# The sine product of the key memory in the phase stage: made by POOL instead of DVE

## The chip, the cores and the metric

The kernel runs on one core of a Trainium2 chip. The metric is the device time of one execution in microseconds (us). The engines are called as in the profile: PE (TensorE) with its weight loads PEld, DVE (VectorE), ACT (ScalarE), POOL (GpSimd) and SP (SyncE, which here only starts transfers).

## The reference, cut to what matters

The model has two layers, each with an attention-like and a feed-forward part, over 8 sequences of 1024 positions and 256 channels. The change lies in the third part, which keeps two running sums over positions. With x normalised and `_shift1` moving the positions back by one, it is:

```python
pos_values = x @ Wpv + bpv
pos_mem_cos = cumsum(pos_cos * pos_values, axis=1)
pos_mem_sin = cumsum(pos_sin * pos_values, axis=1)
pos_ret = (pos_cos * pos_mem_cos + pos_sin * pos_mem_sin) / sqrtD
key_ph = tanh(x @ Wk + bk) * pi
key_cos, key_sin = cos(key_ph), sin(key_ph)
kv_values = x @ Wkv + bkv
gh = gelu(concat([x, _shift1(x)]) @ Wg1 + bg1)
value_gates = sigmoid(gh @ Wg2 + bg2)
kv_mem_cos = cumsum(_shift1(key_cos) * kv_values * value_gates, axis=1)
kv_mem_sin = cumsum(_shift1(key_sin) * kv_values * value_gates, axis=1)
gate_cumsum = maximum(cumsum(value_gates, axis=1), 1.0)
kv_ret = (key_cos * kv_mem_cos + key_sin * kv_mem_sin) / (sqrt(gate_cumsum) * sqrtD)
blended = bw[..., 0:1] * pos_ret + bw[..., 1:2] * kv_ret
return x + layernorm(blended) @ Wo + bo
```

The product that the change moves is `_shift1(key_sin) * (kv_values * value_gates)`.

## The kernel before, in words

The program is a row of stages with a barrier between them: normalise, projections, attention, output projection, routing, experts, phases, slots, combine. Only `phases` is changed (tag `ph`, lines 1394 to 2054). It runs from about 2972 to 3561 us of the profiled span.

In `phases` the 256 channels lie on the partitions in two halves (`mo` = 0 and 1) and the 1024 positions of one sequence `p` along the free dimension, so most tiles are 128x1024 in f32. Each engine has its own instruction order, written out by hand in program order; semaphores tie the engines together, and there is no planner.

- PE makes every projection into four PSUM tiles X, Y, Z, W, used in turn (`products_of` and `SPREAD` fix which product goes into which). `arrived` waits for a product, `gone` waits until its reader has freed it.
- ACT applies gelu, sigmoid, tanh and sine, the roots, and the normalisation of the output.
- DVE does all else: `rotate` (position values times cosine and sine), `key_values` (line 1875 writes `kvg`, the gated values; line 1881 writes `ka` = `kvg` times cosine; line 1882 writes `kb` = `kvg` times sine), `centre` (line 1947), `scan_positions` (lines 1887 and 1888), `scan_keys` (lines 1893 and 1894), `turn_back`, `sum_up` (line 1923 writes the blended result), `gate_sums` (line 1930), `value_weight` (line 1938), and `outputs`, `statistics`, `scales` (line 1982) for the sequence before.
- POOL sets a few constants at the start (lines 1586 to 1592) and then does nothing in the stage.

DVE's order within one pass `p` of its loop (lines 2026 to 2054) is: rotate and key values of half 0, centre of sequence p-1, position scans and key scans of half 0, outputs and statistics of p-1, turn_back of half 0, scales of p-1, sum_up of half 0; then rotate, key values, position scans and key scans of half 1, gate_sums of p+1, turn_back and sum_up of half 1, value_weight of p+1. For p = 0 the half 0 is done ahead of the loop, where no `centre` stands between its products and its key scans. The last pass has neither gate_sums nor value_weight.

A *turn* below is the stretch of DVE from one `value_weight` (line 1938) to the next. Turn p does both halves of sequence p. Turns 1 to 6 begin at 3068.96, 3137.23, 3202.74, 3266.61, 3332.12 and 3395.71 us, and turn 7 at 3459.39 us. Turn 0 is what lies before turn 1, from the gated values at 3021.42 us on.

PE begins its part of a turn with `mean`, whose input is the blended result of line 1923 of the turn before. Behind it PE does `outA`, `outB`, `var`, `k1`, `gh0` and so on without going back to DVE's order. Two things that DVE waits for come down this way: ACT's root of line 1790, which `scales` needs, stands in ACT's order behind the key functions of half 1 and behind `gh0`; ACT's gate values `gt` (line 1738), which `gate_sums` needs, stand behind PE's gate product.

Of the kernel before, what the change touches and what calls it, by code (L numbers as in the profile page):

```python
# [9 lines left out]
ALU = mybir.AluOpType  # L10
# [4 lines left out]
B, T, D = 8, 1024, 256  # L15
NT = T // P
TILES = B * NT
KD = D // P
# [8 lines left out]
FLOOR = 1  # L27
# [1366 lines left out]
def phases(nc, xnT_d, x_d, ppT_d, cols_d, wpv, wk, wkv, wg1, wb1, wo, ident_d, out_d, xn3_d, xnT3_d):  # L1394
# [30 lines left out]
    with Stage(nc, "ph") as st:  # L1425
# [20 lines left out]
        kc = [st.sb(f"kc{mo}", [P, 1 + T]) for mo in range(KD)]  # L1446
        ks = [st.sb(f"ks{mo}", [P, 1 + T]) for mo in range(KD)]
        kvg = st.sb("kvg", [P, T])
        pa = st.sb("pa", [P, T])
        pb = st.sb("pb", [P, T])  # L1450
        ka = st.sb("ka", [P, T])
        kb = st.sb("kb", [P, T])
# [36 lines left out]
        k_ready = st.sem("k_ready")  # L1489
# [4 lines left out]
        w1_ready = st.sem("w1_ready")  # L1494
        rotated = st.sem("rotated")
        m_ready = st.sem("m_ready")
        pos_scanned = st.sem("pos_scanned")
        kv_scanned = st.sem("kv_scanned")
        pos_turned = st.sem("pos_turned")
# [4 lines left out]
        blended = st.sem("blended")  # L1504
# [17 lines left out]
        def arrived(eng, product):  # L1522

            eng.wait_ge(made[bank[product]], FLOOR + turn_of[product] + 1)

        def gone(eng, product):

            eng.wait_ge(freed[bank[product]], FLOOR + turn_of[product] + 1)

        with st.block() as block:  # L1530
# [52 lines left out]
            @block.gpsimd  # L1583
            def _(pool):
                for j in range(2):
                    pool.memset(xT[j][:, :, 0:1], 0.0)
                for mo in range(KD):
                    pool.memset(kc[mo][:, 0:1], 0.0)
                    ins = pool.memset(ks[mo][:, 0:1], 0.0)
                ins.then_inc(zeroed, 1)  # L1590
                pool.memset(avg[:], 1.0 / D)
                pool.memset(avg16[:], 1.0 / D / 16).then_inc(zeroed, 1)

            @block.tensor
            def _(pe):
# [258 lines left out]
            def _(dve):  # L1854
# [12 lines left out]
                def key_values(mo, p):  # L1867

                    u, name = 2 * p + mo, f"kv{mo}"
                    arrived(dve, (name, p))  # L1870
                    if mo == 0:
                        gone(dve, ("gate", p))
                    if u >= 1:
                        dve.wait_ge(m_ready, FLOOR + u)
                    STT(kvg[:], flat[bank[name, p]], column(BKV + mo), gt[:], ALU.add, ALU.mult
                        ).then_inc(freed[bank[name, p]], 1)
                    gone(dve, (name, p))
                    dve.wait_ge(k_ready, FLOOR + u + 1)
                    if u >= 1:
                        dve.wait_ge(blended, FLOOR + u)  # L1880
                    dve.tensor_tensor(ka[:], kvg[:], kc[mo][:, 0:T], ALU.mult)
                    dve.tensor_tensor(kb[:], kvg[:], ks[mo][:, 0:T], ALU.mult).then_inc(m_ready, 1)

                def scan_positions(mo, p):

# [4 lines left out]
                def scan_keys(mo, p):  # L1890

                    dve.wait_ge(m_ready, FLOOR + 2 * p + mo + 1)
                    dve.tensor_tensor_scan(ka[:], ones[:], ka[:], 0.0, ALU.mult, ALU.add)
                    dve.tensor_tensor_scan(kb[:], ones[:], kb[:], 0.0, ALU.mult, ALU.add).then_inc(kv_scanned, 1)

                def turn_back(mo, p):
# [124 lines left out]
                scan_positions(0, 0)  # L2021
                gate_sums(0)
                key_values(0, 0)
                scan_keys(0, 0)
                value_weight(0)
                for p in range(B + 1):
                    if 1 <= p < B:
                        rotate(0, p)
                        key_values(0, p)
                    if p >= 1:  # L2030
                        centre(p - 1)
                    if 1 <= p < B:
                        scan_positions(0, p)
                        scan_keys(0, p)
                    if p >= 1:
                        outputs(p - 1)
                        statistics(p - 1)
                    if p < B:
                        turn_back(0, p)
                    if p >= 1:  # L2040
                        scales(p - 1)
                    if p < B:
                        sum_up(0, p)
                        rotate(1, p)
                        key_values(1, p)
                        scan_positions(1, p)
                        scan_keys(1, p)
                    if p + 1 < B:
                        gate_sums(p + 1)
                    if p < B:  # L2050
                        turn_back(1, p)
                        sum_up(1, p)
                    if p + 1 < B:
                        value_weight(p + 1)
# [431 lines left out]
def build_program(nc, a, out):  # L2486

    def scratch(name, shape):
        return nc.dram_tensor(name, shape, F32, kind="Internal").ap()

    x0, ident = a["x"], a["ident"]
    xn, xnT = scratch("xn", (B * T, D)), scratch("xnT", (KD, P, B * T))
    xn3, xnT3 = scratch("xn3", (B * T, D)), scratch("xnT3", (KD, P, B * T))
    qk, v, ctxT = scratch("qk", (B, 2, H, HD, T)), scratch("v", (B * T, D)), scratch("ctxT", (B, D, T))
    den, rden = scratch("den", (B, H, T)), scratch("rden", (B, H, T))
    x1, x3 = (scratch(n, (B * T, D)) for n in ("x1", "x3"))
    wt = scratch("wt", (P, 2, B * E))
    idx = nc.dram_tensor("idx", (P, 2, B * E), U32, kind="Internal").ap()
    y = scratch("y", (B, NP, D))
    lg = scratch("lg", (B * T, NP))  # L2500

    normalise(nc, "n0", x0, None, xnT, ident)
    qkv_rope(nc, xnT, a["wqk"], a["bqk"], a["L0_attn_Wv"], a["L0_attn_bv"], a["cos"], a["sin"], qk, v)
    attend(nc, qk, v, ident, a["kaug"], ctxT, den, rden)
    project(nc, "pj", ctxT, a["L0_attn_Wo"], a["L0_attn_bo"], x0, x1)
    normalise(nc, "n1", x1, xn, xnT, ident)
    route(nc, xnT, a["L0_ffn_gate_w"], ident, a["rowbase"], idx, wt)
    experts(nc, xn, idx, wt, a["L0_ffn_Wg"], a["L0_ffn_Wu"], a["L0_ffn_Wd"], ident, a["L1_attn_Wo"], a["L1_attn_ln_b"],
            a["L1_attn_bo"], x1, xnT)
    phases(nc, xnT, x1, a["ppT"], a["cols"], *(a["L1_attn_" + n] for n in ("Wpv", "Wk", "Wkv", "Wg1", "Wb1", "Wo")), ident,  # L2510
           x3, xn3, xnT3)
    soft_slots(nc, xn3, xnT3, a["phi"], a["L1_ffn_W"], a["L1_ffn_b"], y, lg)
    soft_combine(nc, lg, y, ident, x3, out)
# [29 lines left out]
```

## Time and profile before

| | us |
|---|---|
| median of 3 runs | 5219.01 |
| lowest, highest | 5214.22, 5226.11 |
| the profiled execution, its own time | 5225.51 |
| its span | 5223.7 |

| engine | busy us | share of the span |
|---|---|---|
| PE | 4665.9 | 89% |
| PEld | 3086.4 | 59% |
| DVE | 3280.5 | 63% |
| ACT | 2126.9 | 41% |
| POOL | 1122.6 | 21% |

A busy share is a mean over stages with different limits, so the table doesn't say what bounds the phase stage; its own stretches do. In the rows below, a timeline row gives start and duration, and in brackets how long the engine sat idle before the instruction and whose work ended that. A row without brackets began without such a wait. An `x8` or `x2` at its end means that so many instructions were merged into the row. PEclk is TensorE's granted clock as a share of full speed.

### The profile page before, as it was taken

To read this page: it belongs to the slowest core of one execution; us is meant where nothing else is said; L and a number is where in the kernel's file an instruction comes from. 1 tells how busy PE (TensorE), PEld (TensorE's weight loads), DVE (VectorE), ACT (ScalarE), POOL (GpSimd) and SP (SyncE) were. 2 spreads that over 40 slices of the span, in tenths; PEclk is the share of its full clock that TensorE was granted. 3 is DMA by queue.
4 is the path that set the end of the run, shared out by engine and by line. 5 is a ranking of instruction groups with operands and counts; after the bars stand their busy time and mean duration, and the time that the engine had idled before them with its cause. 6 is when DMAs were issued, how large, how long until landed. Compare 5 with 4: busy or idle time off the path is not lost. (4 is left out here: it accounts for less than half of the span.)

```text
span 5223.7 us, 71222 instructions
## 1 busy us (share of the span) xinstructions
PE 4665.9 (89%) x27922; PEld 3086.4 (59%) x28080; DVE 3280.5 (63%) x3853; ACT 2126.9 (41%) x3473; POOL 1122.6 (21%) x850
## 2 busy tenths in 40 slices
PE   5969999999999965399999699976999999979999
PEld 3512222222322234288888445446999999968888
DVE  5668888888888814612222389994776666644443
ACT  1027767776766721022222255542222222223333
POOL 1431222122122020044444100001333333310000
PEclk9969999999999985599999899988999999989999
DMA  6644434443443268053434312217444444455553
GB/s 217 186 74 64 63 66 77 73 79 64 72 84 62 36 190 308 30 150 80 88 80 89 103 48 81 81 65 213 100 98 98 101 99 98 98 164 188 187 174 121
DMA packets 458704, 568.05 MB, mean 109 GB/s; under 512 B 29793, under 2 KB 373217, under 8 KB 450017
## 3 DMA queue, kind: packets, MB, share of 16 engines
q1 hardware_dynamic: 261728, 405.44, 29.9%
q10 hardware_dynamic: 172160, 125.85, 10.3%
q0 software_dynamic: 24576, 33.57, 3.9%
q8 instruction: 150, 2.46, 0.2%
q14 instruction: 90, 0.73, 0.1%
HBM read 286.74 MB, written 227.67 MB: 98 GB/s over the span
## 5 line engine op out<-in xcount | busy, mean ns | idle before, releaser
L743 DVE TENSOR_REDUCE att_nmx<-att_s 128x1 f32<-128x1024 f32 x1024 | 1205.4, 1219 | 237.8 <-PE att_s L653 234.1
L729 ACT ACTIVATE att_pt<-att_sT 128x512 f32<-128x512 f32 x2048 | 1059.4, 604 | 481.5 <-PE att_sT L670 307.2
L653 PE MATMUL att_s<-att_KT,att_QT 96*128 96x512 bf16 x2048 | 793.0, 391 | 65.2 <-DMA att_KT<-att_hi 37.8
L670 PE MATMUL att_sT<-att_QT,att_KT 128*128 128x512 bf16 x1890 | 720.6, 384 | 6.8 <-ACT att_pt L729 6.7
L2156 POOL TENSOR_TENSOR sl_lg<-sl_lg,sl_sm 128x512 f32<-128x512 f32 x256 | 319.6, 1269 | 1319.8 <-DVE sl_sm L2294 1319.8
L670 PEld LDWEIGHTS att_sT<-att_QT,att_KT 128*128 128x128 bf16 x2048 | 197.7, 97 | 652.8 <-ACT att_pt L729 441.5
L684 PE MATMUL att_o<-att_pt,att_va 128*32 128x512 f32 x4096 | 555.4, 609 | 0.0
L2167 PE MATMUL sl_lp<-sl_phi,sl_xT 128*128 (+1 forms) x4160 | 491.8, 277 | 31.9 <-DMA sl_xT<-xnT 24.0
L2167 PEld LDWEIGHTS sl_lp<-sl_phi,sl_xT 128*128 128x128 f32 x4160 | 479.2, 193 | 38.8 <-issue 38.8
L2407 PE MATMUL cb_op<-cb_y,cb_exT 128*128 128x256 f32 x2048 | 485.5, 380 | 0.0
L2205 PE MATMUL sl_acc<-sl_lg,sl_xn 128*128 128x128 f32 x4096 | 478.3, 275 | 0.0
L2205 PEld LDWEIGHTS sl_acc<-sl_lg,sl_xn 128*128 128x128 f32 x4096 | 467.7, 192 | 0.0
L2227 ACT ACTIVATE sl_lg<-sl_lg 128x1024 f32<-128x1024 f32 x128 | 135.3, 1057 | 763.5 <-DVE sl_lg L2283 763.5
L1356 DVE TENSOR_TENSOR moe_hT<-moe_sg,moe_up 128x512 f32<-128x512 f32 x128 | 88.0, 688 | 533.5 <-PE moe_yp L1221 325.4
L2407 PEld LDWEIGHTS cb_op<-cb_y,cb_exT 128*128 128x128 f32 x2048 | 370.8, 191 | 40.0
L653 PEld LDWEIGHTS att_s<-att_KT,att_QT 96*128 96x128 bf16 x2048 | 199.1, 99 | 247.3 <-DVE att_nmx L743 50.6
L2292 DVE TENSOR_REDUCE sl_sm<-sl_lg 128x128 f32<-128x1024 f32 x128 | 248.6, 1942 | 136.5 <-ACT sl_lg L2227 136.5
L1154 POOL DMA_INDIRECT x<-moe_y,moe_idx x128 | 213.2, 1666 | 345.0 <-ACT moe_y L1272 325.5
L579 POOL COPY att_QT<-att_QT 32x1024 bf16<-32x1024 bf16 x64 | 72.7, 1162 | 923.1 <-DVE att_QT L764 922.9
L1207 PE MATMUL moe_gp<-moe_xT,moe_wg 128*128 128x256 f32 x1024 | 244.0, 382 | 1.7 <-DVE moe_bo L1374 0.9
L1207 PE MATMUL moe_up<-moe_xT,moe_wu 128*128 128x256 f32 x1024 | 243.1, 380 | 0.0
L1221 PE MATMUL moe_yp<-moe_wd,moe_hT 128*128 128x256 f32 x1024 | 231.6, 379 | 1.4 <-DVE moe_hT L1356 1.4
(251 smaller groups left out, 5985.4 us busy)
## 6 DMA issues: line engine op xcount, KB each, us to landing
lg<-sl_raw ACTq DMA_DIRECT2D x128, 512.0 KB, 5.7
cb_ex<-lg SPq DMA_DIRECT2D x64, 1024.0 KB, 6.2
sl_w<-in_L_ffn_W SPq DMA_DIRECT2D x68, 256.0 KB, 3.7
xnT<-n_xnT ACTq DMA_DIRECT2D x32, 512.0 KB, 5.0
qk<-qkv_turned ACTq DMA_DIRECT2D x64, 256.0 KB, 3.2
att_qin<-qk SPq DMA_DIRECT2D x64, 256.0 KB, 9.1
y<-sl_y SPq DMA_DIRECT2D x16, 1024.0 KB, 7.3
cb_y<-y SPq DMA_DIRECT2D x8, 2048.0 KB, 8.5
```

Of the source, the lines that this page charges most:

```text
L653: ins = pe.matmul(s[i % 2][:, c, :], QT[n % NB][0:ROWS, h, t * P:(t + 1) * P], KT[n % NB][0:ROWS, h, c * 512:(c + 1) * 512], start=True, s ...
L670: pe.matmul(sT[:, idx % 3, :], KT[g % NB][:, h, kt * P:(kt + 1) * P], QT[g % NB][:, h, step // 4 * 512:(step // 4 + 1) * 512], start=True, ...
L684: ins = pe.matmul(o[32 * h:32 * h + 32, :], va[g % 2][:, kt, h, :], pt[:, step % 2, h, c, :], start=kt == 0, stop=kt == NT - 1)
L729: act.activation(pt[:, step % 2, h, c, :], sT[:, idx % 3, :], ACT.Exp, scale=HD ** -0.5).then_inc(exp_done, 1)
L743: dve.tensor_reduce(nmx[n % 2][:, t, h:h + 1], s[i % 2][:].rearrange("p c k -> p (c k)"), AX.X, ALU.max, negate=True).then_inc(freed, 1)
L1207: ins = pe.matmul(o_[:, m, :], w_[:, k, (2 * h + m) * P:(2 * h + m + 1) * P], xT[n % 2][:, k, :], start=k == 0, stop=k == KD - 1)
L1221: ins = pe.matmul(yp[n % 2][:, s, :], hT[m // 2][:, m % 2, s * P:(s + 1) * P], wd[e][:, m, :], start=m == 0, stop=m == NI - 1)
L2156: pool.tensor_tensor(part_, part_, sm[j][:].rearrange("p (a n) -> p a n", a=1).broadcast_to([P, HB, P]), ALU.mult).then_inc(shared, 1)
L2167: ins = pe.matmul(lp[j][:, b, :], xT[:, k, b * T + m * P:b * T + (m + 1) * P], ph[:, k, bass.ds(c * P, P)], start=k == 0, stop=k == KD - 1)
L2205: ins = pe.matmul(acc[:, k, b, :], xn[:, b * NT + m, k * P:(k + 1) * P], lg[m % 4][:, b, :], start=m == 0 and b % 4 == 0, stop=m == NT - 1 ...
L2292: ch.link(dve.tensor_reduce(sm[j][:], lg[l][:].rearrange("p b n -> p n b"), AX.X, ALU.add))
L2407: ins = pe.matmul(op[n % 2][:], exT[n % 2][:, s, :], y[b % 2][:, s, :], start=s == 0, stop=s == SK - 1)
```

## The change

The sine product leaves DVE's `key_values` and becomes POOL's only work in the stage behind its constants. POOL walks through the same sequences and halves. Before each product it waits until `kvg` is written (`gone`), until the keys of this half are ready (`k_ready`), and until `kb` is no longer read (`blended`). It signals a new semaphore, `by_sine`. DVE waits for it ahead of the scan over `kb` and ahead of the next writing of `kvg`.

```diff
+        by_sine = st.sem("by_sine")
...
+                def sine_products(mo, p):
+
+                    u, name = 2 * p + mo, f"kv{mo}"
+                    gone(pool, (name, p))
+                    pool.wait_ge(k_ready, FLOOR + u + 1)
+                    if u >= 1:
+                        pool.wait_ge(blended, FLOOR + u)
+                    pool.tensor_tensor(kb[:], kvg[:], ks[mo][:, 0:T], ALU.mult).then_inc(by_sine, 1)
+
+                for p in range(B):
+                    for mo in range(KD):
+                        sine_products(mo, p)
...
                     if u >= 1:
                         dve.wait_ge(m_ready, FLOOR + u)
+                        dve.wait_ge(by_sine, FLOOR + u)
...
-                    dve.tensor_tensor(ka[:], kvg[:], kc[mo][:, 0:T], ALU.mult)
-                    dve.tensor_tensor(kb[:], kvg[:], ks[mo][:, 0:T], ALU.mult).then_inc(m_ready, 1)
+                    dve.tensor_tensor(ka[:], kvg[:], kc[mo][:, 0:T], ALU.mult).then_inc(m_ready, 1)
...
                     dve.tensor_tensor_scan(ka[:], ones[:], ka[:], 0.0, ALU.mult, ALU.add)
+                    dve.wait_ge(by_sine, FLOOR + 2 * p + mo + 1)
                     dve.tensor_tensor_scan(kb[:], ones[:], kb[:], 0.0, ALU.mult, ALU.add).then_inc(kv_scanned, 1)
```


## Rows read from the trace of the kernel before

**Rows 1.** Turns 2 and 5: us; busy PE, PEld, DVE, ACT, POOL; PEclk; DMA share, GB/s.

```profile
3137.23:3202.74 65.51, 62.59 (x188) 33.67 (x188) 63.41 (x70) 36.17 (x38) 0.00 (x0) 0.95 0.24 81
3332.12:3395.71 63.59, 59.25 (x188) 31.62 (x188) 63.18 (x69) 36.16 (x38) 0.00 (x0) 1.00 0.25 83
```

**Rows 2.** Timeline of PE, head of turn 3: start us, us, engine, line, operation.

```profile
3202.87 2.41 PE L1606 MATMUL ph_psZ<-ph_bl,ph_avg 128*128 128x512 f32 x5 [2.58 <-DVE ph_bl L1923]
```

**Rows 3.** Timeline of DVE: the reciprocal of line 1982, turns 1, 2, 3, 5, 6, 7.

```profile
3102.66 0.20 DVE L1982 RECIPROCAL ph_nrstd<-ph_nrstd 128x8 f32<-128x8 f32 x1 [4.12 <-ACT ph_nrstd L1790]
...
3168.17 0.20 DVE L1982 RECIPROCAL ph_nrstd<-ph_nrstd 128x8 f32<-128x8 f32 x1 [1.34 <-ACT ph_nrstd L1790]
...
3232.25 0.20 DVE L1982 RECIPROCAL ph_nrstd<-ph_nrstd 128x8 f32<-128x8 f32 x1
...
3361.62 0.20 DVE L1982 RECIPROCAL ph_nrstd<-ph_nrstd 128x8 f32<-128x8 f32 x1
...
3425.22 0.19 DVE L1982 RECIPROCAL ph_nrstd<-ph_nrstd 128x8 f32<-128x8 f32 x1
...
3488.90 0.20 DVE L1982 RECIPROCAL ph_nrstd<-ph_nrstd 128x8 f32<-128x8 f32 x1
```

**Rows 4.** Timeline of ACT: the root of line 1790, turns 3, 5, 6, 7.

```profile
3231.70 0.30 ACT L1790 ACTIVATE ph_nrstd<-ph_mv,ph_eps 128x8 f32<-128x8 f32 x1
...
3359.39 0.30 ACT L1790 ACTIVATE ph_nrstd<-ph_mv,ph_eps 128x8 f32<-128x8 f32 x1
...
3424.49 0.30 ACT L1790 ACTIVATE ph_nrstd<-ph_mv,ph_eps 128x8 f32<-128x8 f32 x1
...
3487.88 0.30 ACT L1790 ACTIVATE ph_nrstd<-ph_mv,ph_eps 128x8 f32<-128x8 f32 x1
```

**Rows 5.** Timeline of DVE: the scan of line 1930, turns 1 and 3.

```profile
3123.95 2.29 DVE L1930 TENSOR_TENSOR_SCAN ph_cs<-ph_ones,ph_gt 128x1024 f32<-128x1024 f32 x1 [0.36 <-ACT ph_gt L1738]
...
3253.33 2.29 DVE L1930 TENSOR_TENSOR_SCAN ph_cs<-ph_ones,ph_gt 128x1024 f32<-128x1024 f32 x1 [0.16 <-ACT ph_gt L1738]
```

**Rows 6.** Timeline of DVE, turn 3: start us, us, engine, line, operation.

```profile
3206.26 1.27 DVE L1875 SCALAR_TENSOR_TENSOR ph_kvg<-ph_psX,ph_col,ph_gt 128x1024 f32<-128x1024 f32 x1
3207.57 1.23 DVE L1881 TENSOR_TENSOR ph_ka<-ph_kvg,ph_kc 128x1024 f32<-128x1024 f32 x1
3208.71 1.22 DVE L1882 TENSOR_TENSOR ph_kb<-ph_kvg,ph_ks 128x1024 f32<-128x1024 f32 x1
3209.85 2.34 DVE L1947 SCALAR_TENSOR_TENSOR ph_sq<-ph_bl,ph_psZ 128x1024 f32<-128x1024 f32 x2
3212.11 2.28 DVE L1887 TENSOR_TENSOR_SCAN ph_pa<-ph_ones,ph_pa 128x1024 f32<-128x1024 f32 x1
...
3243.20 1.22 DVE L1882 TENSOR_TENSOR ph_kb<-ph_kvg,ph_ks 128x1024 f32<-128x1024 f32 x1
3244.34 2.28 DVE L1887 TENSOR_TENSOR_SCAN ph_pa<-ph_ones,ph_pa 128x1024 f32<-128x1024 f32 x1
```

**Rows 7.** Timeline, attention stage: POOL and DVE, one stretch.

```profile
709.28 4.50 POOL L599 TENSOR_TENSOR att_num<-att_num,att_rb 128x2048 f32<-128x2048 f32 x1 [31.74 <-DMA att_num<-ctxT]
709.42 4.44 DVE L755 TENSOR_TENSOR att_naug<-att_nrest,att_naug 128x32 bf16<-128x32 f32 x1
```

**Rows 8.** Lines 755 and 579: duration ns min/median/max, first and last start us, forms.

```profile
L755 DVE TENSOR_TENSOR att_naug<-att_nrest,att_naug x32: 226/227/4446, 334.9 to 1818.0; 128x32 bf16<-128x32 f32 x32
L579 POOL COPY att_QT<-att_QT x64: 1034/1078/1317, 338.2 to 1820.8; 32x1024 bf16<-32x1024 bf16 x64
```

**Rows 9.** Group of line 866: busy us, mean ns, idle before.

```profile
L866 POOL TENSOR_TENSOR pj_x<-pj_x,pj_bias 128x1024 f32<-128x1024 f32 x16 | 37.6, 2347 | 41.5 <-DMA pj_x<-in_x 26.8 <-DMA pj_bias<-in_L_attn_bo 14.7
```

**Rows 10.** Timeline, projection stage: DVE and POOL, one stretch.

```profile
98.07 0.74 DVE L333 SCALAR_TENSOR_TENSOR qkv_by_sin<-qkv_mm,qkv_bqk,qkv_sin 128x512 f32<-128x512 f32 x1
98.89 1.26 POOL L350 TENSOR_TENSOR qkv_turned<-qkv_by_cos,qkv_by_sin 128x512 f32<-128x512 f32 x1 [98.43 <-DVE qkv_by_sin L333]
99.42 0.75 DVE L332 SCALAR_TENSOR_TENSOR qkv_by_cos<-qkv_mm,qkv_bqk,qkv_cos 128x512 f32<-128x512 f32 x1 [0.61 <-PE qkv_mm L311]
```

## The prediction, made before the changed kernel was timed

> **What bounds the kernel now.** The page's chain of waits runs only through the combine stage at the end, so for the phase stage I read, in this order: the windows by turn, the waits at the head of a turn, and the places where DVE itself waits. The windows show DVE busy 63.41 of 65.51 us in turn 2 and 63.18 of 63.59 us in turn 5, PE 62.59 and 59.25 us, POOL nothing [rows 1]. DVE is the fuller engine, but PE is close behind, so the second question is who waits for whom. PE stands idle 2.58 us at the head of turn 3, until DVE's blended result is there [rows 2]. So DVE starts each of PE's turns. The other way round, DVE waits twice in a turn for what PE and ACT made from that start: at the reciprocal of line 1982 for ACT's root (4.12 us in turn 1, 1.34 in turn 2, and alike in turn 4; no wait in turns 3, 5, 6, 7) [rows 3], and at the scan of line 1930 for the gate values (0.36 us in turns 1, 2 and 4, 0.16 in turn 3, none in 5 and 6) [rows 5]. There are two loops of nearly one length: DVE's own work, and PE's chain from the blended result to root and gates. A microsecond off DVE counts only where DVE is the later one; a microsecond onto DVE counts nearly everywhere.
>
> How much later DVE is at line 1982 comes from its start less the end of ACT's root and 0.03 us of hand-over (turn 1: 3102.33 + 0.30 to 3102.66): turn 3: 3232.25 - 3232.03 = 0.22 us; turn 5: 1.90; turn 6: 0.40; turn 7: 0.69 [rows 3, 4]. In turns 1, 2 and 4 it is nothing. The gates come 21.3 us behind the root (turn 1: 3123.95 - 3102.66; turn 3: 3253.33 - 3232.03), and DVE needs 20.9 us from line 1982 to line 1930 (21.3 less its wait of 0.36) [rows 3, 5].
>
> **The change part by part.** *Removed from DVE:* 16 products. The next instruction starts 1.14 us behind such a product (3208.71 to 3209.85, 3243.20 to 3244.34) [rows 6], so 2 x 1.14 = 2.28 us a turn.
>
> *Added to POOL:* 16 products of two f32 tiles of 128x1024. The nearest rows are those of line 866, same shape, both inputs f32 in SBUF: 2.35 us each [rows 9]. POOL has nothing else in the stage, so for POOL alone this would be free.
>
> *What the two do to each other.* POOL's 4.50 us product with two SBUF inputs began at 709.28 us. DVE's little product, two SBUF inputs as well, began at 709.42 and took 4.44 us, where its median is 0.227: it ended with POOL's, at 713.8 [rows 7, 8]. So such a DVE instruction does not share; it stands still until POOL is through. The other way, a POOL copy that starts beside a DVE copy takes up to 1.317 us for 1.034, so POOL stands behind a running DVE instruction too [rows 8]. No such loss shows where DVE has one input in PSUM: its multiply of 0.74 us takes 0.75 beside POOL's product [rows 10]. The Trainium skill (SBUF — State Buffer, Who interferes with whom) says the same, and more widely: any DVE instruction with two SBUF inputs contends with a GpSimd instruction that reads SBUF, and the later one to issue is blocked whole. By that rule the scans, which read `ones` and the product, are blocked too; no row of before has a scan beside POOL.
>
> *Who comes first.* DVE's cosine product starts 0.04 us behind the end of `kvg` (3206.26 + 1.27 to 3207.57) [rows 6]; POOL starts 0.08 us behind a DVE result (98.07 + 0.74 to 98.89) [rows 10] and has three waits to go through. So I take DVE as first: POOL's product starts to run when the cosine product ends, 1.2 us later.
>
> *Half 0, turns 1 to 7.* Behind the cosine product come the two instructions of `centre`, with one input in PSUM, 2.26 us until the next starts (3209.85 to 3212.11) [rows 6]. POOL's 2.35 us, of which some 0.1 passes while it stands in line, lie beside them. Cost about nothing, at most 0.1 us; without that cover it would be the 1.2 us of half 1. DVE reaches line 1982 by 1.14 us sooner, and what is late there next is ACT's root: only 0.22 + 1.14 + 0.40 + 0.69 = 2.45 us of the gain are kept, in turns 3, 5, 6, 7, and nothing in 1, 2, 4.
>
> *Half 1, turns 0 to 7, and half 0 of turn 0.* Nothing from PSUM stands between: the cosine product is followed by scans back to back, all with two SBUF inputs [rows 6]. POOL's 2.3 us have to be inserted somewhere in DVE's row: ahead of the first scan if POOL gets its turn there, or at the new wait ahead of the scan over `kb`, where a hand-over of 0.08 us comes on top. Behind the waiting scan stand gate_sums, turn_back, sum_up, and with them PE's next `mean`. Cost: 2.3 - 1.14 = 1.2 us, nine times, 10.8 us. Bounds: if the scans don't contend, it is a gain of 1.14; if POOL ran beside DVE's cosine product, it would end 2.43 us behind `kvg`, 1.2 behind that product, and the cost would be 0; with all of POOL's row and slow hand-overs 1.4.
>
> From the nine come off the waits at line 1930 that are filled: 3 x 0.36 + 0.16 = 1.24 us.
>
> *Other added work.* DVE's wait ahead of `kvg` is for a product scanned long before. One more semaphore is raised by POOL at the stage's start: under 0.1 us. Nothing but DVE reads `kb`, and no transfer moves.
>
> Sum: 10.8 - 2.45 - 1.24 = +7.1 us. The profiled execution's own time of 5225.5 would be 5232.6; it lies 6.5 us above the median of the runs, and 5219.0 + 7.1 = 5226 us.
>
> The size hangs on PE's clock. Turn 5, all at full granted clock, gets the root early; turn 2, at 0.95, gets it 1.34 us later than DVE is ready for it, and is 1.9 us longer [rows 1, 3]. If every turn went like 2, the kept gains and slacks of turns 3, 5, 6, 7 would be gone and the sum would be about +15 us; if every one went like 5, about 0. PE's idle time at a turn's head grows from 2.58 to some 3.4 us, which speaks more for the upper side.
>
> **The rivals.**
>
> *POOL first (slower).* If POOL begins ahead of the cosine product at half 0, DVE stands still for its whole 2.35 us there and `centre` hides nothing. DVE then comes to line 1982 by 1.2 us later instead of 1.14 sooner. It decides where PE's chain leaves less than that: in turns 3, 5, 6 and 7 (in 1 and 2 the waits of 4.12 and 1.34 cover it). There the kept 2.45 us turn into losses of nearly 1.2 each: 7.1 + 2.45 + 4.6 = +14 us, 5233 us. For it: the two starts are only 0.04 us apart. Against: POOL's three waits, and DVE's smaller hand-over.
>
> *The scans don't contend.* The sine product is wholly hidden, DVE gains 2.28 us a turn. But PE's chain holds: nothing is gained in turns 1, 2, 4, next to nothing in 3 and 6 (DVE now comes to line 1930 with no or a little wait), 1.5 in turn 5 (1.90 less the 0.4 by which 21.3 exceeds 20.9), 0.69 + 1.14 in turn 7, and up to 2.3 in turn 0: -5.5 us, 5213.5 us. For it: no row shows a scan beside POOL. Against: it has two SBUF inputs like the blocked product. A scan also takes 2.2 us where a product takes 1.14 [rows 6], so it might read only half the time and leave room in between; nothing shows that. The Trainium skill (DVE: opcode table, instruction layouts, handler registers and perf-mode slots; Datapath and trigger behaviour) has the scan run at half throughput, with which these two times agree.
>
> *POOL runs beside the cosine product.* Half 1 costs 0 and the gain of half 0 is kept only in turns 5 and 7: 1.1 + 0.7, so -2 us, 5217 us. Against: the delayed copies of rows 8.
>
> **How the numbers follow.** Forecast 0.60, POOL first 0.13, scans free 0.13, side by side 0.14. A measurement of this kernel can tell 0.2%, 10.4 us, from no change. The forecast's own range is 5219 to 5234 us by the clock term; within it I give slower by over 0.2% (above 5229.4) a quarter, 0.15. Of POOL first two thirds are slower, 0.09. Of the scans' case, a third with PE's idle time and clock going its way would reach below 5208.6: 0.04, and 0.01 more for the rest. So faster 0.05, same 0.71, slower 0.24. The runs of before alone spread over 12 us, so the range goes from 5211 to 5238.
>
> **What would show it.** After: line 1882 gone from DVE, 16 POOL rows out of `kvg`; at half 0 of turns 1 to 7 a POOL row of about 3.4 us (1.1 in line, 2.3 of work) with `centre` at 2.35 as before; at half 1 either a first scan of 4.5 us instead of 2.28, or a gap of about 2.4 us on DVE ahead of the scan over `kb`, released by POOL. DVE's wait at line 1982 should now appear in all turns but about one or two, the waits at line 1930 should be gone, and turns should be about 0.8 us longer at the same clock. I am wrong if DVE's scans keep 2.2 us beside a running POOL product, if the cosine product takes 3.5 us, or if the phase stage gets shorter by more than 5 us.

## The result and the profile after

The changed kernel took 5224.8 us (median of 22 runs, 5216.4 to 5236.0), the kernel before 5211.6 us in its 22 (5206.6 to 5226.1; the three runs shown first were high for it). The ratio is 1.0027, interval 1.002 to 1.0034, which is 14 us (10 to 18). The profiled execution of after took 5224.59 us, that of before 5225.51, so the two traces hardly differ in length and can only show the mechanism, not the size.

The windows of two turns of after answer to [rows 1]: turn 2 (the common kind) and turn 4 (TensorE at full granted clock all through). Columns as there.

```profile
3130.47:3194.70 64.23, 60.76 (x188) 32.26 (x188) 63.16 (x68) 36.16 (x38) 6.79 (x2) 0.97 0.25 82
3262.28:3325.75 63.47, 59.07 (x188) 31.69 (x188) 63.06 (x68) 36.16 (x38) 6.79 (x2) 1.00 0.25 83
```

POOL is busy 6.79 us a turn, yet DVE's busy time at full clock went only from 63.18 to 63.06 us, although two products of 1.22 us had left it. The busy share doesn't tell work from standing still: a blocked instruction counts as busy. The timeline of after shows where the removed time went. These are half 1 of turn 3 and half 0 of turn 4, to be read beside [rows 6]; the POOL rows are put behind DVE's of the same place.

```profile
3236.99 1.22 DVE L1895 TENSOR_TENSOR ph_ka<-ph_kvg,ph_kc 128x1024 f32<-128x1024 f32 x1
3238.13 4.43 DVE L1900 TENSOR_TENSOR_SCAN ph_pa<-ph_ones,ph_pa 128x1024 f32<-128x1024 f32 x1
3242.49 2.26 DVE L1901 TENSOR_TENSOR_SCAN ph_pb<-ph_ones,ph_pb 128x1024 f32<-128x1024 f32 x1
...
3237.03 3.38 POOL L1601 TENSOR_TENSOR ph_kb<-ph_kvg,ph_ks 128x1024 f32<-128x1024 f32 x1 [34.05 <-DVE ph_kvg L1889]
...
3267.11 1.23 DVE L1895 TENSOR_TENSOR ph_ka<-ph_kvg,ph_kc 128x1024 f32<-128x1024 f32 x1
3268.25 2.34 DVE L1961 SCALAR_TENSOR_TENSOR ph_sq<-ph_bl,ph_psZ 128x1024 f32<-128x1024 f32 x2
3270.51 2.28 DVE L1900 TENSOR_TENSOR_SCAN ph_pa<-ph_ones,ph_pa 128x1024 f32<-128x1024 f32 x1
...
3267.15 3.41 POOL L1601 TENSOR_TENSOR ph_kb<-ph_kvg,ph_ks 128x1024 f32<-128x1024 f32 x1 [26.74 <-DVE ph_kvg L1889]
```

In both halves the POOL product begins 0.04 us behind the cosine product and lasts 3.4 us: one part in line behind it, the rest at work. In half 1 the next DVE instruction is a scan with two SBUF inputs. It takes 4.43 us for 2.28, because it stands still until POOL is through, and the next scan can only start 4.36 us behind it instead of 2.20. In half 0 the next one is `centre`, which reads PSUM; it keeps 2.34 us, and the scan behind it keeps 2.28. The per-line rows say that this is so throughout (duration ns min/median/max):

```profile
L1900 DVE TENSOR_TENSOR_SCAN ph_pa<-ph_ones,ph_pa x16: 2280/3357/4443, 2998.2 to 3493.9; 128x1024 f32<-128x1024 f32 x16
L1906 DVE TENSOR_TENSOR_SCAN ph_ka<-ph_ones,ph_ka x16: 2256/2260/4327, 3019.4 to 3500.5; 128x1024 f32<-128x1024 f32 x16
```

The median of line 1900 lies midway between the two durations: eight scans are long, eight short. Of line 1906 one is long, that of half 0 of sequence 0. That makes the nine collisions of the prediction.

What DVE gains in half 0 shows mostly as a wait. Over the stage it waits at the reciprocal seven times in after where before it was four times [rows 3]. The total hardly differs (7.4 for 7.2 us), because it depends on how many turns ran at a lower clock in that execution; the number of waits tells more. At the gates' scan all waits of [rows 5] are gone; what is left is the one in the stage's head. PE's `mean` at the head of a turn [rows 2] waits longer, 46.4 us for 40.7 over eight. First before, then after (the columns are us in total, times, longest):

```profile
DVE ph_cs L1930 <- ACT ph_gt L1738: 8.5, 5, 7.3
DVE ph_nrstd L1982 <- ACT ph_nrstd L1790: 7.2, 4, 4.1
PE ph_psZ L1606 <- DVE ph_bl L1923: 40.7, 8, 19.0
...
DVE ph_cs L1944 <- ACT ph_gt L1751: 6.7, 1, 6.7
DVE ph_nrstd L1996 <- ACT ph_nrstd L1803: 7.4, 7, 4.0
PE ph_psZ L1619 <- DVE ph_bl L1937: 46.4, 8, 20.0
```

### The profile page after: what moved, and what is told of

The parts are those of the page before. It is cut to its first block and busy times, and to the rows that moved or that the text cites. A ratio compares the mean times of both kernels' runs of the same rounds, so it can differ in the third digit from the quotient of the medians.

```text
span 5222.5 us, 71246 instructions
## 1 busy us (share of the span) xinstructions
PE 4657.3 (89%) x27922; PEld 3084.2 (59%) x28080; DVE 3279.4 (63%) x3837; ACT 2126.6 (41%) x3473; POOL 1176.8 (23%) x866
```

## The experiments

Times below are compared in two ways. The ratio is to runs of before that were timed beside each group of experiments. The second way uses `b1` and `b2`, copies of the kernel before run as experiments: they read 1.0010 and 1.0018 instead of 1.000, so the ratio flatters before by about 7 us. Part of it can be seen: the runs of before lie at two levels. Beside `b2` six of its 29 took 5219.7 to 5225.6 us and the other 23 took 5205.6 to 5215.0, while all eleven of `b2` took 5218.4 to 5229.2. What decides between the levels isn't known. Means over all runs in experiments: copies of before 5223.3 us (22 runs), changed kernel 5227.7 us (24 runs). Differences of means to those 22 runs are called *like for like*; their 95% intervals come from resampling the runs. `b1`, `e4`, `e5` and `e7` ran on one chip, all others, `b2` among them, on another.

**a1_change_again and a2_change: the changed kernel, no edit.**

> The changed kernel once more, for a second profile and for times beside the kernels sent with it. Blocking theory: each POOL product that meets scans stops DVE for about 2.1 us where the removed product took 1.1, so nine times +1.0 us, less what waits on PE and ACT absorb: +5 to +10 us on before by this account, of which the first measurement (+13, interval 10 to 18) shows more. Clock theory: the rest of the +13 comes from more turns in which TensorE's granted clock falls; then this profile has two or more turns of the phase stage longer than 65.5 us. Layout theory: the rest comes from outside the phase stage; then the phase stage from the first gated values to the last blended result takes 498 to 500 us as in both first profiles.

> The changed kernel, to be read against b2_before in the same call and with as many runs, since a copy of the kernel before, sent as an experiment, read 1.0010 and not 1.000. Blocking theory with the measured 1.0 us a collision: +5 to +9 us against b2_before. If the first +13 was right as it stood: +11 to +16 against b2_before.

Measured: 5227.1 us, ratio 1.0024 (1.0015 to 1.0033), and 5229.5 us, 1.0024 (1.0015 to 1.0032). Like for like +4.5 us (1.8 to 7.1) for both together; the 22 runs of the first measurement, taken the same way, give +3.3 (0.4 to 6.2). Against `b2` alone, as a2's expectation had it, a2 is +3.7 us (0.3 to 6.9): the centre lies below the expected +5 to +9, and the +11 to +16 of the other case is out. From the first gated values to the last blended result the three profiles of the change took 498.4, 501.9 and 505.4 us, mean 501.9. The three of before average 499.5 (below), so the stage shows +2.4, with a spread of 7 between executions; the six profiled executions as a whole show +5.5, with a spread of as much. So most of the first +13 came from what it was compared with, and the layout theory has little left to explain; e1 below tests it.

**b1_before_again and b2_before: the kernel before, no edit.**

> The kernel before, sent as an experiment, for a second profile and as a null comparison. The first profile of before was taken at 5225.5 us, 14 above the median of its runs. Clock theory: a run at the median has nearly only turns of 63.6 us in the phase stage, where the first profile had one of 68.3 and two of 65.5; so a profile nearer 5212 shows fewer long turns, and ratio 1.000. Layout theory: the phase stage takes the same 498 to 499 us in it and the difference lies in other stages.

> The kernel before, sent as an experiment once more, as the ruler for the other three. Ratio to the runs of before 1.000 to 1.001.

Measured: 5224.1 us, 1.0010 (1.0001 to 1.0019), and 5224.9 us, 1.0018 (1.001 to 1.0027). A copy of the kernel before reads slower than the kernel before, so a ratio of this size can't be taken as the size of a change. The same stretch of the phase stage took 498.7, 499.7 and 500.0 us in the three profiles of before, with turns of 63.6 to 63.9, 65.5, 67.0 and 68.0 to 68.3 us mixed differently each time. The clock theory says that an execution at the median of 5212 us would be nearly free of long turns. No execution that fast was profiled: b1's took 5221.0 us and had three of them, as many as the first, at 5225.5. The theory stays open.

**e1_signals: all waits and signals, no product on POOL.**

```diff
-                    pool.tensor_tensor(kb[:], kvg[:], ks[mo][:, 0:T], ALU.mult).then_inc(by_sine, 1)
+                    pool.sem_inc(by_sine, 1)
...
-                    dve.tensor_tensor(ka[:], kvg[:], kc[mo][:, 0:T], ALU.mult).then_inc(m_ready, 1)
+                    dve.tensor_tensor(ka[:], kvg[:], kc[mo][:, 0:T], ALU.mult)
+                    dve.tensor_tensor(kb[:], kvg[:], ks[mo][:, 0:T], ALU.mult).then_inc(m_ready, 1)
```

> POOL goes through all its waits and raises by_sine at once, but multiplies nothing; DVE makes both products as in the kernel before and keeps the added waits. Blocking theory: no difference from before (within 3 us), scans 2.27 us, the product of line kb back on DVE. Layout theory (the added waits, the new semaphore or the longer program cost the time): +8 to +14 us as in the changed kernel.

Measured: 5223.0 us, 1.0016 (1.0007 to 1.0024). By the ratio alone this looked like most of the loss. Like for like it is -0.4 us (-2.4 to 2.1): waits, signals and program length cost nothing that these runs can tell. The scans keep their time (first scan 2282 ns on average).

**e2_half0 and e3_half1: only the products of one half on POOL.** The edit chooses by a condition, and DVE makes the others:

```diff
+        by_pool = lambda mo, p: mo == 0 and p >= 1      # e3_half1: mo == 1
+        pool_units = [(mo, p) for p in range(B) for mo in range(KD) if by_pool(mo, p)]
...
+                    if not by_pool(mo, p):
+                        ins = dve.tensor_tensor(kb[:], kvg[:], ks[mo][:, 0:T], ALU.mult)
```

> POOL makes the sine product only for half 0 of sequences 1 to 7, where centre with its PSUM input follows; DVE makes the other nine. Blocking theory: no scan is stopped, POOL rows of 3.4 us beside centre, DVE 1.14 us earlier at the reciprocal of nrstd, where it waits for ACT in nearly all turns: -1 to -3 us on before (kept gain 2.45 by the first profile). Rival (DVE alone sets the turn): 7 x 1.14 = -8 us. Rival (PE's chain sets all): 0.

> POOL makes the sine product only for half 1 of all eight sequences, where scans follow; DVE makes the half-0 ones. Blocking theory: first position scan of half 1 takes 4.4 us instead of 2.28, 8 x 1.0 us less up to 1.2 absorbed at the gates' scan: +6 to +8 us on before, so the whole loss of the changed kernel (and a little more, as half 0's gain is missing) sits here. Rival (the loss is spread over all sixteen products, by waits and signals): half of it, +6 us with e2 also at +5 or more.

Measured: e2 5219.1 us, 1.0006 (0.9996 to 1.0016), like for like -4.3 us (-8.5 to -0.1). e3 5234.3 us, 1.0035 (1.0025 to 1.0045), like for like +9.7 us (5.8 to 13.2). The two halves have opposite signs, as the blocking theory says, and the spread-out rival falls. The times of e2 alone are weak evidence, since five of its twelve runs lie at 5209.7 to 5214.3 us and the other seven at 5218.4 to 5229.6; its turns say more, and e3's interval is clear of 0. The per-line row of e3 has the eight long scans, and none at the key scans, as sequence 0's half 0 is back on DVE:

```profile
L1907 DVE TENSOR_TENSOR_SCAN ph_pa<-ph_ones,ph_pa x16: 2280/3358/4444, 3000.8 to 3504.1; 128x1024 f32<-128x1024 f32 x16
L1913 DVE TENSOR_TENSOR_SCAN ph_ka<-ph_ones,ph_ka x16: 2257/2260/2291, 3023.4 to 3510.6; 128x1024 f32<-128x1024 f32 x16
```

In e2 a turn at full granted clock took 62.45 us, where before took 63.59 [rows 1]: the whole 1.14 us is kept. A turn at 0.95 took 65.33 for 65.51, and one at 0.92 took 67.02 for the 67.04 of `b2`. There DVE waits at the reciprocal, 14.5 us over the stage, twice as long as in before: most of the 8.0 us taken off it is handed to that wait (in this execution, the slowest of e2's twelve). Columns as in [rows 1]:

```profile
3202.79:3265.24 62.45, 59.07 (x188) 31.68 (x188) 62.04 (x69) 36.18 (x38) 3.41 (x1) 1.00 0.25 84
3137.46:3202.79 65.33, 62.41 (x188) 33.64 (x188) 62.25 (x69) 36.17 (x38) 3.41 (x1) 0.95 0.24 81
```

```profile
L2004 DVE RECIPROCAL ph_nrstd<-ph_nrstd 128x8 f32<-128x8 f32 x8 | 1.6, 199 | 14.5 <-ACT ph_nrstd L1806 14.5
```

**e5_both_make: POOL's product comes on top, saving nothing.** The product goes into a tile that nothing reads, and DVE makes both of its own:

```diff
+        idle = st.sb("idle", [P, T])
...
+                    pool.tensor_tensor(idle[:], kvg[:], ks[mo][:, 0:T], ALU.mult).then_inc(by_sine, 1)
```

> DVE makes both products as before, and POOL makes the sine product once more into a tile that nobody reads, with all waits of the changed kernel. This is the cost of POOL's company alone, nothing saved. Blocking theory: POOL is in line behind two DVE products (rows of about 4.5 us), then stops the first scan by 2.1 us in half 1 and in turn 0, is covered by centre otherwise: nine times +2.1 = about +19 us on before, scans of 4.4 us in the same places. Rival (scans share the port): 0.

Measured: one run, 5255.2 us; the stretch of the phase stage took 529.3 us, 30 more than before, where I had expected about 19. The mechanism held, my picture of who waits didn't. I expected POOL in line behind both DVE products and covered by `centre`; the timeline of turn 3 shows it behind the first only:

```profile
3214.78 1.23 DVE L1896 TENSOR_TENSOR ph_ka<-ph_kvg,ph_kc 128x1024 f32<-128x1024 f32 x1
3214.83 3.39 POOL L1602 TENSOR_TENSOR ph_idle<-ph_kvg,ph_ks 128x1024 f32<-128x1024 f32 x1 [27.87 <-DVE ph_kvg L1890]
3215.93 3.37 DVE L1897 TENSOR_TENSOR ph_kb<-ph_kvg,ph_ks 128x1024 f32<-128x1024 f32 x1
3219.22 2.34 DVE L1963 SCALAR_TENSOR_TENSOR ph_sq<-ph_bl,ph_psZ 128x1024 f32<-128x1024 f32 x2
```

DVE's second product takes 3.37 us for 1.22, all sixteen do (mean 3375 ns), and the scans are untouched. So the waiting engine gets its turn at the end of the instruction it waited for, though DVE's next one stands ready. Sixteen times 2.15 is 34 us, less some wait at the gates. In every case seen, the DVE instruction that pays is the one directly behind the cosine product, if both its inputs are in SBUF.

**e7_order_only: the order of e4 on the kernel before.**

```diff
-                        rotate(0, p)
                         key_values(0, p)
+                        rotate(0, p)
...
-                        rotate(1, p)
                         key_values(1, p)
+                        rotate(1, p)
```

> The kernel before with the same reordering as e4_covered (key_values ahead of rotate in both halves from sequence 1 or half 1 on), nothing on POOL. It separates the order from the move to POOL. Blocking theory: 0, within 4 us, since DVE's row is as full as before. Rival (the order itself is what helps or hurts e4_covered): the same sign and size as e4_covered.

Measured: 5226.0 us, 1.0011 (1.0001 to 1.0021), like for like -0.3 us (-4.4 to 3.5). The order alone makes no difference that these runs can tell.

**e4_covered: the change with that order.** The same edit on the changed kernel: behind the cosine product now comes `rotate`, which reads PSUM.

> The change, with key_values ahead of rotate on DVE in both halves (except half 0 of sequence 0), so that DVE's two PSUM-reading products follow the cosine product and POOL's product has them beside it. Blocking theory: scans keep 2.27 us except the first key scan of sequence 0; DVE's own work is 2.28 us a turn shorter than before, but the gate values now bind: a turn at full clock 62.2 us for 63.6, so -5 to -10 us on before, and 15 to 20 us below the changed kernel. Rival (the loss of the change comes from added waits, signals or program length): +5 to +10 us, as POOL and all signals are the same.

Measured: 5219.8 us, 1.0005 (0.9996 to 1.0014), like for like -4.1 us (-6.7 to -1.5), against `b1` alone, on the same chip, -3.0 (-6.2 to 0.6). That is a little short of the expected 5 to 10 below before, and some 8 us below the changed kernel, where I had expected 15 to 20, which fits only the ratio's +13 for the changed kernel. All collisions but sequence 0's half 0 are gone:

```profile
L1900 DVE TENSOR_TENSOR_SCAN ph_pa<-ph_ones,ph_pa x16: 2281/2288/2293, 2997.6 to 3491.6; 128x1024 f32<-128x1024 f32 x16
L1906 DVE TENSOR_TENSOR_SCAN ph_ka<-ph_ones,ph_ka x16: 2261/2265/4336, 3020.3 to 3496.0; 128x1024 f32<-128x1024 f32 x16
...
L1944 DVE TENSOR_TENSOR_SCAN ph_cs<-ph_ones,ph_gt 128x1024 f32<-128x1024 f32 x8 | 18.3, 2288 | 15.5 <-ACT ph_gt L1751 15.5
L1996 DVE RECIPROCAL ph_nrstd<-ph_nrstd 128x8 f32<-128x8 f32 x8 | 1.6, 201 | 10.3 <-ACT ph_nrstd L1803 10.3
```

DVE now stands 25.8 us at the two places that PE's chain feeds, where it was 8.5 + 7.2 in before. The turn at full clock was 61.98 us for 63.59, so there 1.6 of the 2.28 us taken off DVE are kept.

**e8_covered_chain and e9_chain_only: PE's chain shortened, with and without POOL.**

```diff
-                + [(n, p + 1) for n in ("gh1", "bh") if ahead] + [(n, p - 1) for n in ("trA", "trB") if last]
-                + [(n, p + 1) for n in ("gate", "z", "k0", "kv0", "pv0") if ahead])
+                + [(n, p + 1) for n in ("gh1", "bh", "gate") if ahead] + [(n, p - 1) for n in ("trA", "trB") if last]
+                + [(n, p + 1) for n in ("z", "k0", "kv0", "pv0") if ahead])
...
-                    if p + 1 < B:
-                        front("gh0", p + 1)
                     if p >= 1:
                         norm_deviation(p - 1)
                         normal(p - 1)
                     if p + 1 < B:
+                        front("gh0", p + 1)
                         front("gh1", p + 1)
                         front("bh", p + 1)
+                        gates(p + 1)
                     if p >= 1:
                         take_turned(p - 1)
                     if p + 1 < B:
-                        gates(p + 1)
                         shares(p + 1)
```

In PE's own loop `gate(p + 1)` moves ahead of the two `turn` calls in the same way. e8 has beside it the order of e4, and leaves the sine product of sequence 0's half 0 to DVE.

> As e4_covered, with half 0 of sequence 0 left to DVE (nothing from PSUM to cover it), and with PE's chain shortened: PE's gate product ahead of the two transposes, ACT's root and normalisation ahead of the gelu of gh0, ACT's gates ahead of the copies of the transposes. Two-loops theory (what POOL saves on DVE was eaten by the root and the gates that come down PE's chain): DVE's waits at the reciprocal and at the gates' scan all but vanish, a turn is 61.4 us of DVE's own work for 63.6, -12 to -20 us on b2_before. Rival (PE itself, 60 us busy in a turn, or its clock is the floor): turns stay at 62 to 65 us, -3 to -8 us as e4_covered.

> The kernel before with the shortened chain of e8_covered_chain alone, POOL idle. Two-loops theory: DVE's 63.5 us are now the length of every turn, the longer ones of 65.5 and 67 to 68 us go: -4 to -9 us on b2_before. Rival (PE's clock makes the turn long whatever DVE waits for): 0, and long turns remain.

Measured: e8 5190.6 us (5 runs, 5187.9 to 5200.1), ratio 0.9947 (0.9935 to 0.996), like for like -31 us (-35 to -27). It beats both kernels, and by more than the expected 12 to 20. e9 5218.9 us, 1.0003 (0.9994 to 1.0011), like for like -6.3 us (-9.7 to -3.0). e9 is as expected (4 to 9 below). Against `b2` alone, as the expectations had it, they are -32 and -7.5 us. Two turns of e8, turn 3 of e9, and e8's two waits over its stage:

```profile
3127.64:3189.09 61.45, 60.53 (x188) 32.56 (x188) 61.01 (x67) 34.78 (x38) 6.80 (x2) 0.97 0.26 86
3189.09:3252.16 63.07, 62.23 (x188) 33.15 (x188) 61.13 (x68) 34.71 (x38) 6.79 (x2) 0.95 0.25 84
...
3196.40:3260.00 63.60, 62.37 (x188) 33.71 (x188) 63.19 (x70) 34.79 (x37) 0.00 (x0) 0.95 0.25 83
```

```profile
L1951 DVE TENSOR_TENSOR_SCAN ph_cs<-ph_ones,ph_gt 128x1024 f32<-128x1024 f32 x8 | 18.2, 2272 | 8.7 <-ACT ph_gt L1754 8.7
L2003 DVE RECIPROCAL ph_nrstd<-ph_nrstd 128x8 f32<-128x8 f32 x8 | 1.6, 198 | 0.4 <-ACT ph_nrstd L1806 0.4
```

Five of e8's six full turns are 61.4 us, DVE's own work, as expected. The sixth, turn 3 at a granted clock of 0.95, is 63.1 with PE busy 62.2 of it: there PE's work is nearly the whole turn, as the rival had it, and the wait at the gates that is left (1.5 us there, the rest in the head of the stage) is its sign. In e9 five of six are 63.6 us, that of 0.95 too, where before took 65.51 at 0.95. So the long turns of before weren't set by PE's clock alone, but by the waits that a slower PE put into DVE. That is also why my 12 to 20 us was too low: it compared 61.4 with the 63.6 of a good turn, but before's six full turns average 65.2 us in its three profiles, and e8's 61.7.

The two gains are not additive: e4 alone saves 4, the chain alone 6, both 31. The phase stage accounts for the profiled execution: from first gated values to last blended result it took 475.5 us, 24 less than the 499.5 of before's three profiles, and the execution as a whole, 5200.1 us, is 23 below the mean of theirs (5223.4). It was the slowest of e8's five; the other four, 5187.9 to 5192.6 us, have no profile, so where their further 7 to 12 us come from isn't known.

## Why the prediction was right, and where it wasn't

- *POOL's product and DVE's two-input instructions exclude each other, scans too:* right, by after, e3 and e5. The rival that scans are free is out, and so is the one that POOL runs beside the cosine product: its row would then be 2.35 us long [rows 9], and all 16 are 3.38 to 3.41.
- *DVE goes first, POOL starts when the cosine product ends:* right, in all 16, by 0.04 to 0.05 us. POOL got there sooner than I thought, so its three waits cost nearly nothing and the margin is thin. What POOL first would cost was not tried.
- *Half 0 of turns 1 to 7 is covered by `centre`:* right; where DVE doesn't wait, it comes to the reciprocal 28.37 us into the turn for 29.51, exactly the 1.14 saved.
- *Collision +1.2 us:* mis-sized. In the stretch from the reciprocal to the gates' scan DVE needs 21.86 us in after for 20.84 in before, so +1.02. I had 2.3 us of POOL work in DVE's way; the scan is 2.15 us longer. Nine times that is 9.2, not 10.8, and the sum would have been +5.5.
- *The gain is handed to the wait on ACT's root:* right as a mechanism (e2, after): with the chain shortened the same DVE time comes back (e8).
- *The sum, +7.1 us:* like for like +4.5 (1.8 to 7.1); by the given ratio +14 (10 to 18). Turn by turn at the same clock the difference is 67.6 for 67.0, 64.2 for 63.7, 63.5 for 63.6, and in turn 0 49.4 for 47.5 us; that is 1.9 and some 0.4 for most of the others, near 5. I had foreseen 0.8 for a turn; at full clock it is -0.1, as half 0 keeps its whole 1.14 and half 1 costs 1.02. The slacks I read off turns 3, 5, 6 and 7 were one execution's mixture of clocks; in the other profiles of before the waits fall in turns 1, 4 and 5. The same reckoning there gives kept gains of 3.8 and 2.9 us for my 2.45, so the size was near, but it was not a property of those turns.
- *The time, 5226 us:* that 5224.8 was measured is luck in part. I added +7.1 to 5219.0, the median of three runs that was 7.4 above the median of the 22. The measured difference between the two medians is 13.2, so the base was too high by about as much as the difference was too low.
- *The chances:* no change had 0.71. The comparison made first says slower by 0.27%, beyond the 0.2% of the prediction; like for like it is slower by 0.09%, within it. The step that was too sure was taking a bound of 0.2% as clear of noise, when a copy of a kernel can read 0.18% above its original.
- *The clock term, about 15 us if all turns go like turn 2:* open, and its two ends don't follow from the terms named for them: 7.1 plus the kept 2.45 and the slacks of 3.2 is 12.8, not 15; and with 1.14 kept in all seven turns 10.8 - 8.0 is 2.8, not 0. PE's idle time at the head of a turn grew from 2.58 to 3.12 us, and long turns (over 65.4 us) were one, two and three in after's three profiles, three, three and three in before's. The guess that more idle time gives more long turns has no support here.

## What to carry to other kernels

Before moving an elementwise product from DVE to POOL, look at the DVE instructions that follow the moment POOL becomes ready, for as long as POOL will work. In this kernel two of them with one input in PSUM (2.3 us together) covered a POOL product of 2.3 us, and the move was free; where one with two SBUF inputs came first, DVE paid 2.15 us to save 1.14. Putting PSUM readers there cost nothing that could be measured (e7). A single PSUM reader, shorter than POOL's work, was not tried. Then look for the second loop. Here most of the time taken off the fuller engine was eaten by waits that the other engine's chain put into it: both edits together gave 31 us, each alone 4 and 6.

## What the runs showed of the hardware

- A POOL product of two f32 tiles of 128x1024 in SBUF and a DVE scan of the same shape hardly overlap, although the scan takes 2.18 us for 1024 columns where a product takes 1.14: the scan beside POOL took 4.43 us for 2.28. By the rule of the Trainium skill (SBUF — State Buffer, Who interferes with whom) the second of the two to issue blocks whole until the first has finished; the traces agree with it for scans as for products.
- The turn passes to the waiting engine between two DVE instructions issued back to back, in all 16 cases of e5 (mean of the blocked product 3375 ns) and at the nine places of after.
- Beside a DVE instruction with one input in PSUM nothing is lost: the two of `centre` kept 2.34 us, and in e4 `rotate` in their place left all scans but one at 2.26 to 2.29 us.
- A POOL product of 2.35 us alone [rows 9] shows as 3.4 us when it waits for a DVE product; its row alone doesn't say that it waited.
- The same kernel, timed as before and as an experiment, differed by 0.10% and 0.18%, both intervals clear of 1.
- With PE's order and work unchanged, a turn of before took from 63.6 to 63.9 us, at a granted clock of 0.97 to 1.00 of the full 2.4 GHz, over 65.5 (0.95) and 67.0 (0.92) to 68.3 (0.91), in different turns from one execution to the next.
